# Splitting the third expert weights into fp16 pairs once, inside the attention loop, in place of once for every expert tile

## The chip, the cores and the metric

The kernel runs on one core of a Trainium2 chip. The metric is the device time of one execution in microseconds (us). The engines are named as in the profile: PE (matmul), PEld (PE's weight loads), DVE (vector), ACT (scalar), POOL (GpSimd) and SP, which here only issues DMAs. A name with q behind it (PEldq, SPq) is an engine's sequencer.

## The reference, cut to what matters

Two layers follow each other on x of 4 x 256 tokens x 256 features. The first mixes the features with a recurrence, then runs attention with 16 heads, then a mixture of 8 experts of which each token takes 2. The second mixes again and runs a quantised feed-forward block. The part that the change is about is the mixture:

```python
for e in range(E):                      # 8 experts, FF = 896, D = 256
    we = jnp.sum(gates * (top_idx == e), axis=-1)
    ye = jax.nn.silu(ht @ w1[e]) * (ht @ w3[e]) @ w2[e]
    out = out + we[:, None] * ye
```

The product with w2 is done in fp16 halves: 64 * w2 is cut into a high part, rounded to fp16, and a low part, the rest in fp16. The activations are cut likewise, and three of the four products of halves are added in PSUM.

## The kernel before

Every engine has its program written out by hand, in order, with semaphores between engines. The stages that matter here follow each other in time.

**Attention** (from about 113 to 310 us). `attention_steps` runs `step(u)` for u = 0 to 37 on PE, ACT, DVE and POOL. One step works on several units at once, a unit being a head for a pair of batches: in step u PE projects unit u (`proj`), makes the scores of unit u-2, transposes the probabilities of unit u-4 (`prob_transposes`), multiplies unit u-5 with its values (`weighted_values`) and projects unit u-6 out (`project_out`). ACT in step u does `exponentials(u-3)`, `pT_high(u-4)`, `swap_halves(KU+u)`, `o_high(u-5)`, in this order; DVE does `rope(KU+u)`, `normalise(u-3)`, `row_max(u-2)`, `pT_low(u-4)`, `o_low(u-5)`. PE's `proj` of step u+1 waits for `swap_halves` of step u, since both use the bank pb[0]. In steps 0 to 3 ACT and DVE also split wo.

**Routing** (to about 343 us), and then the **experts** (to about 580 us). The tokens are sorted into MT = 23 tiles of 128 slots; tile n belongs to expert e, read from a table in SBUF at run time (`tile_base`, `value_load`). The three weights of an expert lie as fp32 in one of RING = 3 places of `wreg`, loaded by `load_expert` on SP. For tile n PE does `up` (both first products, in two parts), `h_transposes(n-1)`, `x_transposes(n+1)` and `down(n-1)`. `w2_high` on ACT and `w2_low` on DVE split w2 of the tile's expert into `w2s`, for each of the 23 tiles, two buffers in turn. Beside its tile work DVE does pieces of the second layer's recurrence and of its weights (`beside_a`, `beside_b`), and POOL gathers rows and feeds the recurrence.

SP's own order is: the inputs, wo (after the first weights are split), `load_expert(0)` after wo is split, the stores of h2, experts 1 and 2, then the rest as tiles end.

Of the kernel before, what the change touches and what calls it, by code (L numbers as in the profile page):

```python
# [14 lines left out]
P = 128  # L15
# [23 lines left out]
SCALE = float(HD) ** -0.5  # L39
BLK = 3 * P  # L40
# [23 lines left out]
def build(nc, t, out):  # L64
    ctx = ExitStack()
    with ctx:
        def sb(name, shape, dt=F32):
            return ctx.enter_context(nc.sbuf_tensor(name, shape, dt))
# [54 lines left out]
        def recurrence_buffers(base):  # L123
# [14 lines left out]
        w2s = [[cut(region, at, FC * D // 2, F16).rearrange("p (c n) -> p c n", c=FC) for region, at in parts]  # L138
               for parts in (((areg, 4224), (areg, 5120)), ((areg, 6016), (breg, 5120)))]
# [83 lines left out]
        row_ids = sb("row_ids", [P, MT], I32)  # L223
        h2_dram = nc.dram_tensor("h2_dram", (NT * P, D), F32).ap()
# [22 lines left out]
            "hT_done hT_copied hTlo_done w2hi_done w2lo_done down_done y_copied "  # L247
# [18 lines left out]
        def load_expert(eng, e):  # L266

            base = (e % RING) * WEXP
            n = C * FF
            eng.dma_start(wreg[:, base:base + n].rearrange("p (c n) -> p c n", c=C),  # L270
                          t["L0_ffn_w1"][e].rearrange("(c p) n -> p c n", p=P)).then_inc(s_w[e % RING], 16)
            eng.dma_start(wreg[:, base + n:base + 2 * n].rearrange("p (c n) -> p c n", c=C),
                          t["L0_ffn_w3"][e].rearrange("(c p) n -> p c n", p=P)).then_inc(s_w[e % RING], 16)
            eng.dma_start(wreg[:, base + 2 * n:base + WEXP].rearrange("p (c n) -> p c n", c=FC),
                          t["L0_ffn_w2"][e].rearrange("(c p) n -> p c n", p=P)).then_inc(s_w[e % RING], 16)
# [9 lines left out]
        def _(sp):  # L285
# [25 lines left out]

            sp.wait_ge(s["wolo_done"], 4)
            load_expert(sp, 0)
# [49 lines left out]
        def _(pe):  # L363
# [229 lines left out]
            def down(n, parity, piece=None):  # L593
                pe.wait_ge(s["hTlo_done"], n + 1)
                pe.wait_ge(s["w2lo_done"], n + 1)
                if not isinstance(n, int) or n >= 1:
                    pe.wait_ge(s["y_copied"], n)
                if piece:
                    piece(pw)
                for c in range(FC):  # L600
                    last = split_products(pw[:, 0:D], lambda a: hhT[:, a, c, :], lambda a: w2s[parity][a][:, c, :], c == 0, c == FC - 1)
                last.then_inc(s["down_done"], 1)
# [12 lines left out]
            for n in range(MT + 1):  # L615
                parity = n % 2
                if n < MT:
                    e, base = tile_base(n)
                    pe.wait_ge(s["w_ready"], e + 1)
                    pe.wait_ge(s["xT_copied"], n + 1)  # L620
                    if n >= 1:
                        pe.wait_ge(s["inner_a_done"], n)
                    up(n, parity, base, 0)
                if n >= 1:
                    h_transposes(n - 1)
                if n + 1 < MT:
                    x_transposes(n + 1, (n + 1) % 4, x_slot.get(n))
                if n < MT:
                    up(n, parity, base, 1)
                if n >= 1:  # L630
                    down(n - 1, 1 - parity, y_slot.get(n))
# [58 lines left out]
        def _(act):  # L690
# [142 lines left out]

            def step(u, parity):
# [8 lines left out]
                if u < 4:  # L843
                    wo_high(u)
                if H + LAG + 1 <= u < H + LAG + 5:
                    squares_of_tile(u - H - LAG - 1)
# [51 lines left out]
            def w2_high(n, parity):  # L898

                e = act.value_load(tmi[0:1, bass.ds(n, 1)], min_val=0, max_val=NE - 1)  # L900
                act.wait_ge(s["w_ready"], e + 1)
                if not isinstance(n, int) or n >= 2:
                    act.wait_ge(s["down_done"], n)
                nc.scalar.activation(w2s[parity][0].rearrange("p c n -> p (c n)"),  # L904
                                     wreg[:, bass.ds((e % RING) * WEXP + 2 * C * FF, FC * D)], ACT.Copy, scale=WS).then_inc(s["w2hi_done"], 1)

# [6 lines left out]
            for n in range(MT + 1):  # L913
# [17 lines left out]
                if n < MT:  # L931
                    w2_high(n, parity)
# [57 lines left out]
        def _(dve):  # L990
# [186 lines left out]

            def second_norm(i):
# [4 lines left out]
            def step(u, parity):  # L1183
# [13 lines left out]
                if u < 4:  # L1197
                    wo_low(u)
                if H + LAG + 3 <= u < H + LAG + 7:
                    second_norm(u - H - LAG - 3)  # L1200
# [173 lines left out]
            def w2_low(n, parity):  # L1374

                e = dve.value_load(tmi[0:1, bass.ds(n, 1)], min_val=0, max_val=NE - 1)
                dve.wait_ge(s["w2hi_done"], n + 1)
                V.scalar_tensor_tensor(w2s[parity][1].rearrange("p c n -> p (c n)"),  # L1378
                                       wreg[:, bass.ds((e % RING) * WEXP + 2 * C * FF, FC * D)], WS,
                                       w2s[parity][0].rearrange("p c n -> p (c n)"), ALU.mult, ALU.subtract).then_inc(s["w2lo_done"], 1)  # L1380

# [14 lines left out]
            for n in range(MT):  # L1396
# [6 lines left out]
                w2_low(n, n % 2)  # L1403
# [287 lines left out]
```

## Time and profile before

| | |
|---|---|
| median of 3 runs | 705.23 us (705.21 to 707.87) |
| the profiled execution, its own time | 705.76 us |
| its span in the trace | 703.9 us |
| PE busy | 503.7 us |
| DVE busy | 539.9 us |
| ACT busy | 342.4 us |

The profiled execution took 705.76 us, of which the trace's span covers 703.9; some 1.9 us lie around it. Busy time is a sum over stages that have different limits, so it has to be read stage by stage.

### The profile page before, as it was taken

How to read it: one execution, taken by the hardware profiler on the slowest of the kernel's cores; microseconds unless marked ns; L12 is line 12 of the kernel's file. 1: busy time of each engine (PE TensorE's matmuls, PEld its weight loads, DVE VectorE, ACT ScalarE, POOL GpSimd, SP SyncE). 2: the span in 40 equal slices, each digit the busy share in tenths (PEclk: the TensorE clock that was granted, in tenths of full speed). 3: DMA queues.
4: the chain of work that ended last, by engine and by line, in shares of the span. 5: the costliest groups of instructions: out<-in, count | busy, mean ns of one | idle time of the engine just before them, and what ended most of it. 6: DMA issues, size and time to landing. Idle time of an engine off the chain costs nothing.

```text
span 703.9 us, 9187 instructions
## 1 busy us (share of the span) xinstructions
PE 503.7 (72%) x2954; PEld 342.0 (49%) x2954; DVE 539.9 (77%) x1004; ACT 342.4 (49%) x737; POOL 287.7 (41%) x232
## 2 busy tenths in 40 slices
PE   2011385799999999983589899999899980363442
PEld 1001132578888788863256566666566650132221
DVE  4999685788888889844288698787976853799983
ACT  3235154677777787830244645456255531342231
POOL 3454035644444455223534855332520004664250
PEclk9999999899999999995699999999999995555555
DMA  9200011400000000009216531604251002010000
GB/s 264 92 0 0 0 55 65 155 4 1 1 1 1 1 17 17 1 31 312 73 31 213 172 46 61 194 27 171 38 180 65 15 16 68 16 52 8 16 16 15
DMA packets 28314, 44.23 MB, mean 63 GB/s; under 512 B 4779, under 2 KB 21419, under 8 KB 28011
## 3 DMA queue, kind: packets, MB, share of 16 engines
q1 hardware_dynamic: 20843, 31.43, 13.8%
q0 software_dynamic: 3024, 8.14, 4.8%
q10 hardware_dynamic: 4400, 4.06, 1.7%
q8 instruction: 25, 0.41, 0.3%
q14 instruction: 22, 0.18, 0.1%
HBM read 38.51 MB, written 5.12 MB: 62 GB/s over the span
## 4 chain that ended last, share of the span: by engine, by line
PE 47%; DVE 30%; issue 10%; ACT 6%; POOL 5%; DMA 1%; SPq 0%; ACTq 0%; DVEq 0%; POOLq 0%
PE pb L405 9%; PE pw L405 9%; PE pb L581 6%; PE sc L444 6%; PE sc L581 5%; PE po L405 4%; PE pt L455 3%; DVE areg L1045 2%; DVE areg L1031 2%; DVE areg L1029 1%; PE pt L590 1%; POOL breg L1583 1%; DVE areg L1042 1%; DVE areg L1286 1%; DVE areg L1378 1%
## 5 line engine op out<-in xcount | busy, mean ns | idle before, releaser
L581 PE MATMUL pb<-wreg,areg 128*128 x184 | 84.8, 604 | 1.1 <-ACT areg L892 0.8
L1555 POOL TENSOR_TENSOR breg<-breg,con 128x512 f32<-128x512 f32 x32 | 40.7, 1270 | 82.9 <-ACT breg L794 82.9
L405 PE MATMUL pb<-areg,wreg 128*128 128x512 f16 x240 | 60.8, 391 | 14.8 <-ACT breg L794 9.4
L405 PE MATMUL pw<-areg 128*128 128x256 f16 x406 | 59.5, 283 | 8.7 <-DVE areg L1386 8.7
L581 PE MATMUL sc<-wreg,areg 128*128 x184 | 63.2, 486 | 0.0
L802 ACT ACTIVATE breg<-breg,mx 128x128 f32<-128x128 f32 (+1 forms) x128 | 56.6, 445 | 1.9 <-DVE mx L1153 1.7
L1597 POOL DMA_INDIRECT areg<-h_dram,row_ids x23 | 32.1, 1396 | 57.9 <-PE po L573 39.9
L581 PEld LDWEIGHTS pb<-wreg,areg 128*128 128x128 f32 x184 | 33.9, 195 | 36.5 <-issue 36.2
L405 PEld LDWEIGHTS pw<-areg 128*128 128x128 f16 x406 | 40.7, 101 | 19.3 <-DVE areg L1386 12.2
L444 PE MATMUL sc<-areg,breg 128*128 128x128 f32 (+1 forms) x256 | 49.5, 338 | 0.4 <-DVE mx L1153 0.4
L1550 POOL TENSOR_TENSOR breg<-breg 128x512 f32<-128x512 f32 x32 | 44.5, 1392 | 4.5
L444 PEld LDWEIGHTS sc<-areg,breg 128*128 128x128 f32 x256 | 40.1, 199 | 7.5 <-issue 1.6
L811 ACT CAST breg<-pt 128x768 f16<-128x768 f32 x32 | 25.5, 798 | 36.5 <-PE pt L455 36.5
L405 PEld LDWEIGHTS pb<-areg,wreg 128*128 128x128 f16 x240 | 22.2, 99 | 41.4 <-ACT breg L794 12.3
L581 PEld LDWEIGHTS sc<-wreg,areg 128*128 128x128 f32 x184 | 33.2, 190 | 18.3
L1153 DVE CUSTOM_DVE_ANT_0 breg<-sc,con 128x128 f32<-128x128 f32 (+1 forms) x128 | 38.1, 354 | 5.0 <-PE pt L455 2.0
L1372 DVE TENSOR_TENSOR areg<-areg,pb 128x512 f32<-128x512 f32 x23 | 15.7, 681 | 32.9 <-ACT areg L922 20.6
L922 ACT ACTIVATE areg<-pb 128x512 f32<-128x512 f32 x23 | 13.8, 598 | 54.6 <-PE pb L581 52.5
L1102 DVE TENSOR_TENSOR breg<-pb,con 128x512 f32<-128x512 f32 x40 | 27.5, 689 | 16.6 <-PE pb L405 14.1
L904 ACT ACTIVATE areg<-wreg 128x1792 f16 x23 | 39.6, 1724 | 0.0
L1643 POOL DMA_INDIRECT areg<-ys_dram,sloti x16 | 15.5, 967 | 55.0 <-DMA ys_dram<-areg 50.7
L382 PE MATMUL sc<-con,areg 128*128 128x128 f32 x16 | 4.5, 434 | 45.8 <-DVE areg L1048 45.8
(237 smaller groups left out, 1336.2 us busy)
## 6 DMA issues: line engine op xcount, KB each, us to landing
wreg<-in_L_ffn_w SPq DMA_DIRECT2D x24, 896.0 KB
ys_dram<-areg ACTq DMA_DIRECT2D x23, 128.0 KB
wreg<-in_L_ffn_wq SPq DMA_DIRECT2D x1, 2048.0 KB, 9.6
wreg<-in_L_ffn_wo SPq DMA_DIRECT2D x1, 2048.0 KB, 8.1
areg<-in_fside_BxSxS ACTq DMA_DIRECT2D x4, 256.0 KB, 5.9
x_in<-in_x SPq DMA_DIRECT2D x4, 256.0 KB, 4.1
h_dram<-areg SPq DMA_DIRECT2D x8, 128.0 KB, 1.9
out_dram<-areg SPq DMA_DIRECT2D x8, 128.0 KB, 1.7
```

Of the source, the lines that this page charges most:

```text
L405: last = nc.tensor.matmul(bank, w(a), m(b), start=first and k == 0, stop=final and k == 2)
L444: last = nc.tensor.matmul(sc2[:, b, o:o + w], qr[:, buf, b * S + qb * P:b * S + (qb + 1) * P], kT[:, kv, pair * PAIR + b * S:pair * PAIR + ...
L455: last = nc.tensor.transpose(pt2[:, b, k * P:(k + 1) * P], pr[:, buf, b, k * P:(k + 1) * P], ident)
L581: last = nc.tensor.matmul(bank, xsT[:, parity, c * P:(c + 1) * P], wreg[:, bass.ds(base + (m * C + c) * FF + lo, w)], start=c == 0, stop=c ...
L802: last = nc.scalar.activation(pr[:, parity, b, o:o + w], pr[:, parity, b, o:o + w], ACT.Exp, bias=mx[:, parity, k:k + 1], scale=-1.0, accu ...
L811: nc.scalar.copy(pT[:, parity, 0], pt2[:, :, 0:BLK]).then_inc(s["pThi_done"], 1)
L904: nc.scalar.activation(w2s[parity][0].rearrange("p c n -> p (c n)"), wreg[:, bass.ds((e % RING) * WEXP + 2 * C * FF, FC * D)], ACT.Copy, s ...
L1102: V.tensor_tensor(t1[:, parity, :].rearrange("p (b n) -> p b n", b=2), bank[:, :].rearrange("p (b n) -> p b n", b=2), rope_cos.rearrange(" ...
L1153: last = V.tensor_tensor_reduce(out=pr[:, parity, b, o:o + w], in0=sc2[:, b, o:o + w], in1=mask[:, o:o + w], scale=-SCALE, scalar=3e38, op ...
L1550: G.tensor_tensor(dst, t1[:, parity, :], t2[:, parity, :], ALU.add).then_inc(s["radd_done"], 1)
L1555: G.tensor_tensor(t2[:, parity, :].rearrange("p (b n) -> p b n", b=2), t2[:, parity, :].rearrange("p (b n) -> p b n", b=2), rope_sin.rearr ...
L1597: G.indirect_dma_start(out=xs[n % 4], out_offset=None, in_=h2_dram[:, :], in_offset=bass.IndirectOffsetOnAxis(ap=row_ids[:, n:n + 1], axis ...
```

## The change

w2 of all 8 experts is split before the experts begin. `W2_STEPS` names the attention steps 6, 8, ..., 20. In step 6 + 2e ACT makes the high half of expert e (`w2_high(e)`), at the end of its step; in step 7 + 2e DVE makes the low half (`w2_low(e)`), at the end of its step. There is one buffer for the fp32 weights (`w2_words`, in `areg`) and one for each half (`w2_half`). SP loads `w2_words` from DRAM, and stores both halves to the new DRAM tensor `w2_dram` once the low half is made; only behind these two stores does it issue the next expert's load. ACT waits for that load (`w2_in`) and for the two stores (`w2_out`) ahead of its next high half. `load_expert` takes the third weight as fp16 pairs from `w2_dram`, the same number of bytes as before, and `load_expert(0)` comes behind all of this on SP. In the expert tiles `w2_high` and `w2_low` are gone, and PE reads the halves where they lie in `wreg`, at an address that depends on the expert.

```diff
+W2_STEPS = tuple(range(6, 6 + 2 * NE, 2))
...
+        w2_words = cut(areg, 11264, FC * D)
+        w2_half = [cut(areg, at, FC * D // 2, F16) for at in (13056, 16896)]
...
-            eng.dma_start(wreg[:, base + 2 * n:base + WEXP].rearrange("p (c n) -> p c n", c=FC),
-                          t["L0_ffn_w2"][e].rearrange("(c p) n -> p c n", p=P)).then_inc(s_w[e % RING], 16)
+            eng.dma_start(cut(wreg, base + 2 * n, FC * D, F16).rearrange("p (s n) -> p s n", s=2), w2_dram[e])\
+                .then_inc(s_w[e % RING], 16)
...
+            for e in range(NE + 1):
+                if e >= 1:
+                    sp.wait_ge(s["w2lo_done"], e)
+                    for k in range(2):
+                        sp.dma_start(w2_dram[e - 1][:, k], w2_half[k]).then_inc(s["w2_out"], 16)
+                elif e == 0:
+                    sp.wait_ge(s["rat_done"], B)
+                if e < NE:
+                    sp.dma_start(w2_words.rearrange("p (c n) -> p c n", c=FC), t["L0_ffn_w2"][e].rearrange("(c p) n -> p c n", p=P))\
+                        .then_inc(s["w2_in"], 16)
             sp.wait_ge(s["wolo_done"], 4)
+            sp.wait_ge(s["w2_out"], 32 * NE)
             load_expert(sp, 0)
...
 # PE, down
-                pe.wait_ge(s["w2lo_done"], n + 1)
...
-                    last = split_products(pw[:, 0:D], lambda a: hhT[:, a, c, :], lambda a: w2s[parity][a][:, c, :], c == 0, c == FC - 1)
+                    last = split_products(pw[:, 0:D], lambda a: hhT[:, a, c, :],
+                                          lambda a: wreg[:, bass.ds(base + 2 * C * FF + (a * FC + c) * D // 2, D // 2)].bitcast(F16),
+                                          c == 0, c == FC - 1)
...
 # ACT
+            def w2_high(e):
+                act.wait_ge(s["w2_in"], 16 * (e + 1))
+                if e >= 1:
+                    act.wait_ge(s["w2_out"], 32 * e)
+                nc.scalar.activation(w2_half[0], w2_words, ACT.Copy, scale=WS).then_inc(s["w2hi_done"], 1)
...
+                if u in W2_STEPS:
+                    w2_high(W2_STEPS.index(u))
...
 # DVE
+            def w2_low(e):
+                dve.wait_ge(s["w2hi_done"], e + 1)
+                V.scalar_tensor_tensor(w2_half[1], w2_words, WS, w2_half[0], ALU.mult, ALU.subtract).then_inc(s["w2lo_done"], 1)
...
+                if u - 1 in W2_STEPS:
+                    w2_low(W2_STEPS.index(u - 1))
```

How the instructions stand, first on ACT, at the end of attention step 8. Before, `o_high` (the CAST out of po) is followed at once by the four ACTIVATE of the next step's `exponentials`; the CAST out of pt is `pT_high`, the two COPY are `swap_halves`:

```order
L817 CAST areg<-po 128x512
L802 ACTIVATE breg,sums<-breg,mx 128x128
L802 ACTIVATE breg,sums<-breg,mx 128x256
L802 ACTIVATE breg,sums<-breg,mx 128x128
L802 ACTIVATE breg,sums<-breg,mx 128x256
L811 CAST breg<-pt 128x768
L793 COPY breg<-pb 64x512
L794 COPY breg<-pb 64x512
```

After, with every line number higher:

```order
L833 CAST areg<-po 128x512
L854 ACTIVATE areg<-areg 128x1792
L818 ACTIVATE breg,sums<-breg,mx 128x128
L818 ACTIVATE breg,sums<-breg,mx 128x256
L818 ACTIVATE breg,sums<-breg,mx 128x128
L818 ACTIVATE breg,sums<-breg,mx 128x256
L827 CAST breg<-pt 128x768
L809 COPY breg<-pb 64x512
L810 COPY breg<-pb 64x512
```

The L854 row is `w2_high`, which waits for the load of `w2_words` and for the stores of the halves; the exponentials and both copies of the next step now stand behind it.

Then PE, in an expert tile. Before, between two parts of `up` (L581), the whole of `down` is one run of 21 matmuls, and the ISA rows, which work out an address in registers, stand only ahead of the matmuls of `up`:

```order
L581 ISA
L581 MATMUL sc<-wreg,areg 128x384
L405 MATMUL pw<-areg 128x256 x21
L610 TENSOR_LOAD tmi
L610 ISA x2
L619 REGISTER_ALU
L581 ISA
L581 MATMUL pb<-wreg,areg 128x512
```

After, the run of `down` (L418) has an ISA row ahead of two of every three matmuls, 14 in a tile; a piece of it and its end:

```order
L594 ISA
L594 MATMUL sc<-wreg,areg 128x384
L418 ISA
L418 MATMUL pw<-wreg,areg 128x256
L418 ISA
L418 MATMUL pw<-wreg,areg 128x256 x2
...
L624 TENSOR_LOAD tmi
L624 ISA x2
L635 REGISTER_ALU
L594 ISA
L594 MATMUL pb<-wreg,areg 128x512
```

What moved here: the reads of `down` go to `wreg`, and 14 register instructions joined PE's sequencer in each tile.

## Rows read from the trace of the kernel before

**Rows 1.** The page: busy time by engine.

```profile
PE 503.7 (72%) x2954; PEld 342.0 (49%) x2954; DVE 539.9 (77%) x1004; ACT 342.4 (49%) x737; POOL 287.7 (41%) x232
```

**Rows 2.** Windows: attention steps 6 to 21, two steps, the expert stage.

```profile
core 0: us, PE busy (x) PEld busy (x) DVE busy (x) ACT busy (x) POOL busy (x), PEclk, DMA share, GB/s
142.53:232.24 89.71, 89.56 (x706) 72.81 (x707) 74.91 (x225) 69.17 (x193) 41.01 (x33) 1.00 0.01 1
170.93:182.05 11.12, 11.12 (x90) 9.07 (x88) 9.32 (x28) 8.60 (x25) 5.07 (x5) 1.00 0.00 0
343.87:580.45 236.58, 224.04 (x1120) 142.38 (x1120) 184.29 (x198) 116.71 (x193) 85.47 (x61) 0.98 0.31 93
```

**Rows 3.** Timeline of ACT in one attention step (start, length, instruction).

```profile
171.17 0.40 ACT L802 ACTIVATE breg<-breg,mx 128x128 f32<-128x128 f32 x1
...
174.23 0.80 ACT L811 CAST breg<-pt 128x768 f16<-128x768 f32 x1 [1.20 <-PE pt L455]
...
176.25 0.58 ACT L817 CAST areg<-po 128x512 f16<-128x512 f32 x1
```

**Rows 4.** Timeline of DVE in the same step.

```profile
173.06 0.18 DVE L1134 RECIPROCAL sums<-sums 128x4 f32<-128x4 f32 x1
...
175.49 0.95 DVE L1160 TENSOR_TENSOR breg<-pt,breg 128x768 f16<-128x768 f32 x1
176.87 0.69 DVE L1164 TENSOR_TENSOR areg<-po,areg 128x512 f16<-128x512 f32 x1 [0.43 <-ACT areg L817]
```

**Rows 5.** The splits of w2, by their lines (ns min/median/max, first and last start).

```profile
L904 ACT ACTIVATE areg<-wreg x23: 1710/1721/1742, 351.5 to 570.2; 128x1792 f16 x23
L1378 DVE SCALAR_TENSOR_TENSOR areg<-wreg,areg x12: 2019/2026/3167, 354.8 to 573.2; 128x1792 f16<-128x1792 f16 x12
```

**Rows 6.** DMA issues (KB each, median us from issue to landing).

```profile
wreg<-in_L_ffn_wo SPq DMA_DIRECT2D x1, 2048.0 KB, 8.1
...
h_dram<-areg SPq DMA_DIRECT2D x8, 128.0 KB, 1.9
```

**Rows 7.** Windows: wo on its way (1 KB rows), then expert weights w1, w3 (3.5 KB rows).

```profile
106.00:107.00 1.00, 1.00 (x6) 0.41 (x6) 0.31 (x1) 0.45 (x1) 0.59 (x1) 1.00 1.09 362
136.00:137.00 1.00, 1.00 (x3) 0.30 (x2) 0.14 (x1) 1.00 (x6) 0.86 (x2) 0.50 1.01 412
```

**Rows 8.** Timeline of PE: waits, and two tiles without one.

```profile
361.36 2.47 PE L405 MATMUL pw<-areg 128*128 128x256 f16 x21 [1.68 <-DVE areg L1386]
402.74 3.77 PE L405 MATMUL pw<-areg 128*128 128x256 f16 x21 [3.34 <-DVE areg L1386]
433.07 0.28 PE L405 MATMUL pw<-areg 128*128 128x256 f16 x1 [0.54 <-DVE areg L1386]
443.44 0.33 PE L552 MATMUL pw<-identb,breg 88*128 88x88 bf16 x4 [0.90 <-DVE areg L1386]
465.02 3.60 PE L581 MATMUL pb<-wreg,areg 128*128 x8
474.31 3.60 PE L581 MATMUL pb<-wreg,areg 128*128 x8
491.75 0.28 PE L405 MATMUL pw<-areg 128*128 128x256 f16 x1 [0.54 <-DVE areg L1386]
503.84 4.13 PE L405 MATMUL pw<-areg 128*128 128x256 f16 x21 [2.62 <-DVE areg L1386]
```

**Rows 9.** Windows: a stretch with PE mostly idle, and the one behind it.

```profile
398.50:402.00 3.50, 0.89 (x3) 0.19 (x1) 1.17 (x2) 3.47 (x8) 3.12 (x3) 1.00 0.01 2
402.00:405.40 3.40, 2.66 (x13) 1.92 (x14) 3.37 (x4) 2.10 (x3) 3.09 (x3) 0.50 0.01 0
```

**Rows 10.** PE's sequencer in two tiles, and the start of one `down`.

```profile
L610 PEldq TENSOR_LOAD <-tmi x2: 298/302/305, 463.1 to 472.4; - x2
L581 PEldq FUSED_REGOPS  x12: 46/46/104, 463.9 to 473.8; - x12
...
472.02 0.27 PE L405 MATMUL pw<-areg 128*128 128x256 f16 x1
```

More of the change, by code:

```diff
@@ L136, in build @@
         hhT = cut(areg, 2816, FF, F16).rearrange("p (s c n) -> p s c n", s=2, c=FC)
-        w2s = [[cut(region, at, FC * D // 2, F16).rearrange("p (c n) -> p c n", c=FC) for region, at in parts]
-               for parts in (((areg, 4224), (areg, 5120)), ((areg, 6016), (breg, 5120)))]
+        w2_words = cut(areg, 11264, FC * D)
+        w2_half = [cut(areg, at, FC * D // 2, F16) for at in (13056, 16896)]
         ysb = cut(areg, 3712, 2 * D).rearrange("p (k n) -> p k n", k=2)
@@ L223, in build @@
         row_ids = sb("row_ids", [P, MT], I32)
+        w2_dram = nc.dram_tensor("w2_dram", (NE, P, 2, FC * D), F16).ap()
         h2_dram = nc.dram_tensor("h2_dram", (NT * P, D), F32).ap()
@@ L246, in build @@
             "w_ready xT_done xT_copied upa_done upb_done silu_a_done silu_b_done inner_a_done inner_b_done "
-            "hT_done hT_copied hTlo_done w2hi_done w2lo_done down_done y_copied "
+            "hT_done hT_copied hTlo_done w2_in w2_out w2hi_done w2lo_done down_done y_copied "
             "x1_ready sgx_ready qx_ready qxT_done qxT_copied gatep_done upp_done gate_ready gsig_ready up_ready p_ready "
@@ L591, in h_transposes, with down @@
                 last.then_inc(s["hT_done"], 1)
-            def down(n, parity, piece=None):
+            def down(n, base, piece=None):
                 pe.wait_ge(s["hTlo_done"], n + 1)
-                pe.wait_ge(s["w2lo_done"], n + 1)
                 if not isinstance(n, int) or n >= 1:
@@ L616, in _ @@
                 parity = n % 2
+                if n >= 1:
+                    last_base = base
                 if n < MT:
@@ L630, in _ @@
                 if n >= 1:
-                    down(n - 1, 1 - parity, y_slot.get(n))
+                    down(n - 1, last_base, y_slot.get(n))
             def quantised_transposes(i):
@@ L896, in _ @@
             copy_xT(0, 0)
[L898 to L905, printed above, removed]
             for k in range(2):
@@ L931, in _ @@
                 if n < MT:
-                    w2_high(n, parity)
                     act.wait_ge(s["upb_done"], n + 1)
@@ L1372, in silu @@
                 V.tensor_tensor(hh[:, lo:hi], silu_out[:, lo:hi], b, ALU.mult).then_inc(done, 1)
[L1374 to L1380, printed above, removed]
             def hT_low(n):
@@ L1402, in _ @@
                 silu(n, 1)
-                w2_low(n, n % 2)
                 if n in beside_b:
```

## The prediction

> **What bounds the kernel now.** I read the busy times of the page first, only to see that no engine limits the whole: PE has 72% and DVE 77% [rows 1]. The windows by stage say more [rows 2]. In attention steps 6 to 21 PE is busy 89.56 of 89.71 us, at the full clock (a granted clock of 1.00, the 2.4 GHz level). Over two steps it is busy 11.12 of 11.12 us, while ACT has 8.60 and DVE 9.32. So PE sets 5.56 us a step there, ACT has 1.26 us free a step and DVE 0.90. In the expert stage PE is busy 224.04 of 236.58 us, and DVE 184.29: PE again, with some 12.5 us of gaps. Two tiles without a gap start 474.31 - 465.02 = 9.29 us apart [rows 8]; 23 such tiles would be 213.7 us, so 22.9 us is all that lies above the barest tile, and part of that is PE's own work for the second layer.
>
> **What leaves the expert tiles.** 23 times 1.72 us of ACT and 23 times 2.03 us of DVE [rows 5], 39.6 and 46.6 us of busy time. Neither engine is the limit, so only PE's gaps count, those behind a DVE chain that holds a `w2_low` [rows 8]. The wait of 1.68 us at 361.36 ends with `hT_low(0)`, behind a `w2_low` of 2.03 on DVE: all of it goes, 1.7. The 3.34 at 402.74 goes back to POOL, whose gather waits for a DVE piece that three splits stand ahead of; POOL would start about 3.7 us earlier, of which the tiles themselves gained 1.7, so 2.0. The small waits, 0.54, 0.90 and 0.54, are shorter than one split: 2.0. The 2.62 at 503.84 lies behind a DVE that never rests and a split that took 3.17 (the longest in [rows 5]), so all goes, and with it the slow `down` behind it: 4.13 us where 2.47 is usual, 1.7, at half clock. Sum 1.7 + 2.0 + 2.0 + 4.3 = 10.0. The bounds are 5 (half of the gaps find another cause at once, above all POOL) and 16 (all 22.9 less the side pieces on PE).
>
> **What joins the expert tiles.** `down` gets 14 address computations a tile. One takes 46 ns on PE's sequencer [rows 10], 0.64 us a tile, 14.8 us in all if it showed. It is covered by the queue between sequencer and array: `down` begins on the array at 472.02, and the sequencer already loads the next tile's number at 472.4, so it had passed all 21 matmuls with about 1.9 us of array work to go. With 0.64 us more it still is ahead by about 1.2. Cost 0; without that cover, 0.64 us and the next tile's look-up of 0.30, for 22 tiles: the bound is 20. The third load has its old size, with longer rows: 0.
>
> **What joins attention.** By busy time the splits nearly fit: 1.72 in ACT's 2.52 free us of two steps, 2.03 against DVE's 1.80, a little over. What matters is the order. `w2_high(e)` needs `w2_words` filled again, and SP issues this load only when `w2_low(e-1)` has ended, behind two stores. That low half is the last thing of DVE's step 5 + 2e, and the high half the last of ACT's step 6 + 2e. DVE ends its step at 177.56 (`o_low`, 176.87 + 0.69) and ACT its own at 176.83 (176.25 + 0.58) [rows 3, 4], so ACT wants the weights 5.56 - 0.73 - 2.03 = 2.8 us after the low half. In this time 0.9 MB have to go out and 0.9 MB to come in.
>
> I build the loop from the end of `w2_high`, as time zero. The four exponentials take 1.89 us up to the reciprocal (171.17 to 173.06). From there to the end of `pT_low` are 3.38 (to 176.44). `o_low` adds 0.69, since `o_high` is done in time: the 0.43 that it waits for now is gone. Together 5.96, and `w2_low` 2.03: 8.0. Then the transfer: wo, 2.10 MB in the same 1 KB rows, landed in 8.1 us [rows 6], and moved 362 GB/s in mid-flight [rows 7]; 2.10 / 0.362 = 5.8, so 2.3 us are fixed. Now 0.917 MB goes out in 3.5 KB rows, which I price like the 3.5 KB rows of w1 and w3 at 412 GB/s, 2.2 us, and 0.917 MB comes in at 362, 2.5 us, in one queue: 2.3 + 2.2 + 2.5 = 7.0, and 0.1 for SP to wake, 7.1. With `w2_high` itself the loop is 8.0 + 7.1 + 1.8 = 16.9 us for two steps where PE needs 11.1. The rest of the loop is covered: ACT reaches the next high half at about 10.5 (the second step's rope waits for `w2_low` until 8.0) and stands still for some 4.7 us.
>
> **Who waits behind it.** Behind the waiting ACTIVATE stand the exponentials and `swap_halves` of the next step; PE's `proj` waits for the swap. PE still finishes one step, then idles 16.9 - 11.1 = 5.8 us a loop. Seven loops, for e = 1 to 7: 7 x 5.8 = 40.6. At the ends the first split delays its steps by about 3 us, and half comes back in steps 22 to 31, where DVE is slower than PE by little: 2.0. `load_expert(0)` moves from 132 us to behind step 21; it has over 60 us to land, so 0.
>
> For the transfer no row shows a store of this size. Below, the load without the stores would be 2.3 + 2.5 = 4.8, and I put the low end at 5.5. Above, both at half the rate make 2.3 + 9.4 = 11.7; the nearest store, 128 KB in 1.9 us [rows 6], has no such slowness, so I take 9.5. Each us is 7 us of the sum.
>
> The Trainium skill, "DMA: Bandwidth & Descriptors", section "Anatomy of one DMA", gives a DMA as about 2.0 us plus its bytes at 436 GB/s. By that the transfer would take 6.2 us, the loop 16.0 and the seven loops 34: an estimate from the page that is 6 us below mine, since wo moved slower than that here. The same section warns that a completion can be late when the target is HBM, which the stores here are. The 1.9 us of a 128 KB store does not bear that out, and no row shows it for 448 KB.
>
> **Sum.** 703.9 + 40.6 + 2.0 - 10.0 = 736.5 of span, 738.4 with the 1.9 us around it. The profiled execution was 0.5 above the median of its runs, so 738.
>
> **The rivals.**
> - *The transfers hide.* If one loop of DMA took 1.3 us or less (11.1 - 8.0 - 1.8), ACT would not wait, and attention would pay only DVE's 0.2 us for two steps, some 3 in all: 705.2 + 3 - 10 = 698, faster. Over it the loss grows by 7 us for each us, and the whole change breaks even near 2.4. Even 128 KB takes 1.9, and here it is fourteen times that. 3 in 100.
> - *Nearly even.* A short transfer (5.5, a loop of 15.3, so 7 x 4.2 = 29.4) and 16 gained in the tiles give 705.2 + 29.4 + 2 - 16 = 720.6, still 2% slower. For within 0.5% the loop would have to be near 13. 3 in 100.
> - *The clock.* When PE had been mostly idle for 3.5 us, the next 3.4 us ran at 0.50 [rows 9], the 1.2 GHz level. A loop has a gap of 5.8 us, so I expect such a stretch in each: it costs PE about 1.7 us of work, which the gap absorbs. If instead the clock stays low through the loop, PE's 11.1 us become up to 22 and PE sets the loop again: 7 x 11.1 - 10 = +68, 773. Against it, PE would be busy for 11 us on end, and the expert stage, which holds such a stretch, has a mean of 0.98 [rows 2]. 6 in 100.
> - *The sequencer shows.* PE's address work costs 0.3 to 0.9 us a tile: 745 to 758. 8 in 100.
> - *A slower or faster transfer.* At 9.5 us 755, at 5.5 us 727. 20 in 100 together.
> - The forecast itself, within 731 to 745: 60 in 100.
>
> **How the numbers follow.** The predicted time is the forecast's. The range takes both ends of the transfer and part of the gain's bounds: 724 to 757. It leaves out the hidden transfers, the even case and the low clock, 12 in 100, and some tails. A measurement of this kernel tells about 0.5%, or 3.5 us, from no change. Faster has the first rival's chance and a little for a gain that I don't see: 0.04; same 0.03; slower 0.93.
>
> **What would show it.** In the profile after: ACT's `w2_high` waits for a DMA seven times, for about 4.7 us each, near 33 in all. Attention's steps 8 to 21 come in pairs 16.9 us apart, at a PE busy share near 66%. The stores and the load land about 7 us after the low half. PE's waits in the expert stage fall from 12.5 to a few us, with `down` still at 2.3 us, and the stage takes about 227. The prediction is wrong if the pairs stay near 11 us, if the sequencer stretches `down` above 2.5 us, or if POOL keeps the gaps of the expert stage.

## The result: 6.1% slower, and where the time went

| | before | after |
|---|---|---|
| median of 4 runs | 706.55 us | 751.07 us (747.49 to 752.36) |
| the profiled execution, its own time | 705.76 us | 749.89 us |
| its span in the trace | 703.9 us | 748.1 us |
| start to the first tile's `up` | 343.87 us | 391.42 us |
| the expert stage | 236.58 us | 233.07 us |
| from its end to the end | 123.45 us | 123.61 us |

The ratio is 1.0614, with a 95% interval of 1.0555 to 1.0673. The span grew by 44.2 us: 47.55 ahead of the experts, -3.5 in their stage, 0.2 behind it. The forecast had 42.6, -10 and 0.

**The loop of two steps.** First the page's line of busy times, against [rows 1], then windows against [rows 2]: all seven loops (from 0.2 us ahead of the end of the first `w2_low` to just behind the end of the last), two single loops, and the expert stage.

```profile
PE 517.9 (69%) x2954; PEld 348.4 (47%) x2954; DVE 511.2 (68%) x989; ACT 320.3 (43%) x722; POOL 277.9 (37%) x232
```

```profile
core 0: us, PE busy (x) PEld busy (x) DVE busy (x) ACT busy (x) POOL busy (x), PEclk, DMA share, GB/s
160.86:282.46 121.60, 89.18 (x601) 68.18 (x599) 79.94 (x205) 70.69 (x174) 35.53 (x28) 0.87 0.32 107
161.06:178.02 16.96, 11.49 (x76) 8.25 (x75) 11.32 (x30) 9.41 (x24) 5.07 (x4) 0.90 0.32 108
178.02:196.17 18.15, 12.58 (x83) 9.45 (x81) 11.34 (x31) 10.21 (x25) 5.08 (x4) 0.82 0.30 102
391.42:624.49 233.07, 225.86 (x1120) 141.70 (x1120) 137.06 (x175) 81.75 (x170) 76.70 (x61) 0.99 0.30 94
```

Where PE was busy for all of 11.12 us, it now has 11.5 to 12.6 us of work in a loop of 17 to 18, some of it at half clock. The sums of busy time fell on DVE (28.7 us) and ACT (22.1 us), and the kernel got slower all the same: the work went, the order stayed in the way.

ACT's waits show the transfer, and the timelines of ACT and DVE the loop around it (start, length, instruction, and in brackets the idle time before it and what ended it). L854 is `w2_high`, L1194 `w2_low`:

```profile
ACT areg L854 <- DMA areg<-in_L_ffn_w: 29.8, 7, 5.4
```

```profile
168.07 1.70 ACT L854 ACTIVATE areg<-areg 128x1792 f16<-128x1792 f32 x1 [4.60 <-DMA areg<-in_L_ffn_w]
...
186.21 1.70 ACT L854 ACTIVATE areg<-areg 128x1792 f16<-128x1792 f32 x1 [5.41 <-DMA areg<-in_L_ffn_w]
203.24 1.70 ACT L854 ACTIVATE areg<-areg 128x1792 f16<-128x1792 f32 x1 [3.15 <-DMA areg<-in_L_ffn_w]
```

```profile
171.55 0.18 DVE L1148 RECIPROCAL sums<-sums 128x4 f32<-128x4 f32 x1 [5.57 <-ACT breg L818]
...
173.81 0.95 DVE L1174 TENSOR_TENSOR breg<-pt,breg 128x768 f16<-128x768 f32 x1
...
175.28 2.74 DVE L1194 SCALAR_TENSOR_TENSOR areg<-areg 128x1792 f16<-128x1792 f32 x1
```

From the start of `w2_high` to the start of `w2_low` are 175.28 - 168.07 = 7.21 us, and in the next loop again (186.21, and a `w2_low` at 193.42). `w2_low` takes 2.74. From its end at 178.02 to the next `w2_high` at 186.21 are 8.19 us, in the loops before and after it 7.01 and 7.07, over the seven 7.38 on average. 7.21 + 2.75 + 7.38 = 17.34 us, and the ends of the first and the eighth `w2_low` say the same: (282.41 - 161.06) / 7 = 17.34. Seven loops cost 7 x (17.34 - 11.12) = 43.5 us, and 4.0 of the 47.55 are left for the ends.

The chain that ended last, cut out around one transfer (start, length, what), names its parts; the groups of DMA issues (KB each, median us to landing) give their usual sizes:

```profile
175.36 2.67 DVE areg L1194
...
178.05 0.32 SPq L318
...
178.41 0.43 SPq L318
...
178.89 7.30 DMA areg<-in_L_ffn_w
```

```profile
areg<-in_L_ffn_w SPq DMA_DIRECT2D x8, 896.0 KB, 6.4
w_dram<-areg SPq DMA_DIRECT2D x16, 448.0 KB, 3.5
```

SP needs 0.85 us to issue both stores (L318), and then the load takes 6.4 as a rule.

PE waits behind it for the swap (ACT L810), in each loop. In four of the seven loops, after waits of 4.76 to 5.57 us, the first six matmuls then run at half clock, 2.74 us where 1.47 is usual. In the other three the wait was 3.31 to 4.04 us, and they take 1.47 to 1.57. Before the first loop and in it:

```profile
162.92 1.47 PE L418 MATMUL pb<-areg,wreg 128*128 128x512 f16 x6 [0.68 <-ACT breg L810]
...
173.45 2.74 PE L418 MATMUL pb<-areg,wreg 128*128 128x512 f16 x6 [4.79 <-ACT breg L810]
```

**The expert stage.** PE's waits in it, and its timeline over two tiles, against [rows 8]; L418 with x21 is `down`, L594 is `up`:

```profile
PE pb L594 <- issue: 1.9, 7, 0.5
PE pw L418 <- DVE areg L1398: 1.7, 3, 0.6
```

```profile
497.08 2.46 PE L418 MATMUL pw<-wreg,areg 128*128 x21
499.38 3.68 PE L594 MATMUL pb<-wreg,areg 128*128 x8
...
506.64 2.46 PE L418 MATMUL pw<-wreg,areg 128*128 x21
509.13 2.41 PE L594 MATMUL pb<-wreg,areg 128*128 x5
```

`down`'s waits for DVE are down to 1.7 us, as forecast, but a new releaser stands there, "issue", 1.9 us in 7 pieces, ahead of the first matmuls of `up`. This tile takes 509.13 - 499.38 = 9.75 us, with four small transposes of the second layer in it. The tile behind it has none of them: it ends with the next start at 518.81 and takes 9.68, where such a tile took 9.29 before. The starts of the tiles now lie 9.6 to 9.8 us apart nearly throughout, three of them 10.6 to 10.8; before, most lay 9.3 to 10.0 apart, by what the second layer adds to each, and three of them 11.2 to 14.3. The long tiles are gone, and each plain one has 0.3 to 0.4 us more. PE's sequencer shows why, against [rows 10]; L418 are the address computations of `down`, L624 is the look-up of the next tile's expert:

```profile
L418 PEldq FUSED_REGOPS  x28: 55/55/60, 506.0 to 517.6; - x28
```

```profile
L624 PEldq TENSOR_LOAD <-tmi x2: 299/304/308, 508.1 to 517.8; - x2
```

The first address of this `down` is worked out at 506.0 and the look-up begins at 508.1. Those 2.1 us hold 14 addresses and 21 weight loads with their matmuls, so each address takes some 0.15 us with the one or two pairs behind it. The look-up begins 1.5 us after the start of `down` (506.64), where it began 0.4 after it before. It ends too late for the first weight load of `up` to go ahead of its matmul: that load starts at 509.12, after 0.31 us in which PEld has nothing, and the matmul at 509.13. Before, they started at 474.20 and 474.31.

### The profile page after: what moved, and what is told of

The parts are those of the page before. It is cut to its first block, busy times and chain, and to the rows that moved or that the text cites. A ratio compares the mean times of both kernels' runs of the same rounds, so it can differ in the third digit from the quotient of the medians.

```text
span 748.1 us, 9271 instructions
## 1 busy us (share of the span) xinstructions
PE 517.9 (69%) x2954; PEld 348.4 (47%) x2954; DVE 511.2 (68%) x989; ACT 320.3 (43%) x722; POOL 277.9 (37%) x232
## 4 chain that ended last, share of the span: by engine, by line
PE 41%; DVE 28%; issue 11%; ACT 8%; DMA 7%; POOL 2%; SPq 1%; ACTq 0%; POOLq 0%; DVEq 0%
PE pb L594 9%; PE pw L418 8%; PE sc L594 7%; DMA areg<-in_L_ffn_w 6%; PE pb L418 5%; PE sc L457 3%; DVE areg L1194 3%; ACT breg L818 2%; PE pt L603 2%; DVE areg L1059 2%; PE po L418 2%; DVE areg L1045 1%; DVE breg L1167 1%; PE pt L468 1%; DVE areg L1043 1%
## 5 line engine op out<-in xcount | busy, mean ns | idle before, releaser
L418 PE MATMUL pb<-areg,wreg 128*128 128x512 f16 x240 | 66.2, 417 | 47.9 <-ACT breg L810 42.7
L418 PE MATMUL pw<-wreg,areg 128*128 (+2 forms) x699 | 89.9, 279 | 3.0 <-DVE areg L1398 1.7
L594 PE MATMUL pb<-wreg,areg 128*128 x184 | 86.2, 612 | 3.7 <-issue 1.9
L418 PEld LDWEIGHTS pw<-wreg,areg 128*128 128x128 f16 x699 | 68.1, 99 | 19.8 <-issue 6.5
L594 PE MATMUL sc<-wreg,areg 128*128 x184 | 63.2, 486 | 0.0
L418 PEld LDWEIGHTS pb<-areg,wreg 128*128 128x128 f16 x240 | 22.8, 103 | 78.2 <-ACT breg L810 47.4
L457 PE MATMUL sc<-areg,breg 128*128 128x128 f32 (+1 forms) x256 | 56.7, 374 | 0.6 <-DVE mx L1167 0.6
L594 PEld LDWEIGHTS pb<-wreg,areg 128*128 128x128 f32 x184 | 33.7, 193 | 43.0 <-issue 42.6
L457 PEld LDWEIGHTS sc<-areg,breg 128*128 128x128 f32 x256 | 45.9, 225 | 9.6 <-issue 3.0
L1608 POOL DMA_INDIRECT areg<-h_dram,row_ids x23 | 27.4, 1190 | 60.5 <-PE po L586 43.1
L1561 POOL TENSOR_TENSOR breg<-breg 128x512 f32<-128x512 f32 x32 | 43.5, 1360 | 4.5
L594 PEld LDWEIGHTS sc<-wreg,areg 128*128 128x128 f32 x184 | 33.2, 190 | 18.3
L937 ACT ACTIVATE areg<-pb 128x512 f32<-128x512 f32 x23 | 13.8, 599 | 62.7 <-PE pb L594 62.7
L418 PE MATMUL po<-breg,areg 128*128 128x256 f16 (+1 forms) x384 | 36.9, 246 | 0.3 <-DVE areg L1178 0.3
L1148 DVE RECIPROCAL sums<-sums 128x4 f32<-128x4 f32 x32 | 5.5, 172 | 45.9 <-ACT breg L818 45.4
```

Source lines behind the costliest of these rows:

```text
L418: last = nc.tensor.matmul(bank, w(a), m(b), start=first and k == 0, stop=final and k == 2)
L457: last = nc.tensor.matmul(sc2[:, b, o:o + w], qr[:, buf, b * S + qb * P:b * S + (qb + 1) * P], kT[:, kv, pair * PAIR + b * S:pair * PAIR + ...
L594: last = nc.tensor.matmul(bank, xsT[:, parity, c * P:(c + 1) * P], wreg[:, bass.ds(base + (m * C + c) * FF + lo, w)], start=c == 0, stop=c ...
L1561: G.tensor_tensor(dst, t1[:, parity, :], t2[:, parity, :], ALU.add).then_inc(s["radd_done"], 1)
L1608: G.indirect_dma_start(out=xs[n % 4], out_offset=None, in_=h2_dram[:, :], in_offset=bass.IndirectOffsetOnAxis(ap=row_ids[:, n:n + 1], axis ...
```

## Experiments

The ratio stands against the kernel before, timed beside them: 708.15 us for the first four, 706.79 for the next two, 706.28 for the last (medians). Where nothing is said of it, a kernel computes all of the reference.

**1. The transfers out of the way.** Two buffers for `w2_words` and two for the halves, in `areg` and in the free first place of `wreg`. SP loads expert e + 2 behind the stores of expert e, so each load has two steps of time.

```diff
-        w2_words = cut(areg, 11264, FC * D)
-        w2_half = [cut(areg, at, FC * D // 2, F16) for at in (13056, 16896)]
+        w2_words = [cut(areg, 11264, FC * D), cut(wreg, 0, FC * D)]
+        w2_half = [[cut(areg, at, FC * D // 2, F16) for at in (13056, 16896)],
+                   [cut(wreg, at, FC * D // 2, F16) for at in (FC * D, FC * D + FC * D // 2)]]
...
+            load_w2(0)
             sp.wait_ge(s["wolo_done"], 4)
+            load_w2(1)
+            for e in range(NE):
+                sp.wait_ge(s["w2lo_done"], e + 1)
+                for k in range(2):
+                    sp.dma_start(w2_dram[e][:, k], w2_half[e % 2][k]).then_inc(s_w2out[e % 2], 16)
+                if e + 2 < NE:
+                    load_w2(e + 2)
```

> The changed kernel with two buffers for the fp32 weights and two for each half, so that the load of expert e + 2 is issued when the low half of e is made, and ACT finds its weights there. The same splits, stores and tiles. Theory A (attention loses its time to the loop from the low half over the two stores and the load to the next high half, 17.3 us in place of 11.1): ACT's waits of 29.8 us go, a pair of steps falls to 11.4 to 12.1 us (DVE has 9.32 of 11.12 us of its own and 2.03 to 2.75 for the split), and the time falls from 751 to 704 to 711, about 708. Theory B (it is the splits' own work on ACT and DVE, or the clock, or the traffic): at least half of the loss stays, 730 or more.

Measured: 713.44 us, ratio 1.0083 (1.0048 to 1.0118). No `w2_high` waits for a DMA any more, and the experts begin at 356.01 instead of 391.42, 35.4 us earlier. So the wait for the transfer is 35.4 of the 47.55 us, which settles the main step. But the time misses theory A's 704 to 711, and a pair of steps its 11.4 to 12.1: 12.1 us of attention's loss are still there. A window of two steps (columns as above), and PE around it (L817 is the second copy of `swap_halves` in this kernel):

```profile
175.00:187.30 12.30, 11.48 (x90) 9.00 (x90) 11.36 (x30) 10.12 (x26) 5.12 (x5) 1.00 0.46 149
```

```profile
185.70 1.47 PE L425 MATMUL pb<-areg,wreg 128*128 128x512 f16 x6 [0.72 <-ACT breg L817]
...
197.99 1.47 PE L425 MATMUL pb<-areg,wreg 128*128 128x512 f16 x6 [0.72 <-ACT breg L817]
```

```profile
ACT breg L816 <- DVE breg L1123: 17.4, 11, 4.9
```

Two steps take 197.99 - 185.70 = 12.29 us, 1.17 over the old 11.12. The swap waits for DVE's rope (L1123), and the rope stands behind a `w2_low` of 2.76 us. Eight pairs at 1.17 are 9.4 of the 12.1.

**2. The addresses alone.** The kernel before, its splits still in every tile, but PE's `down` reads the halves through an address with a register in it. The register is always zero, so the same data are read.

```diff
+            def w2_at(parity, a, c):
+                region, at = (((areg, 4224), (areg, 5120)), ((areg, 6016), (breg, 5120)))[parity][a]
+                return region[:, bass.ds(zero + at + c * D // 2, D // 2)].bitcast(F16)
...
-                    last = split_products(pw[:, 0:D], lambda a: hhT[:, a, c, :], lambda a: w2s[parity][a][:, c, :], c == 0, c == FC - 1)
+                    last = split_products(pw[:, 0:D], lambda a: hhT[:, a, c, :], lambda a: w2_at(parity, a, c), c == 0, c == FC - 1)
...
+                    zero = e * none
```

> The kernel before, with the splits where they were; only, down reads its halves at an address that PE works out in registers (the offset is zero at run time), 14 address computations a tile as in the changed kernel. Theory A (the sequencer shows: in the changed kernel tiles without a wait start 9.7 us apart, not 9.29): tiles without a wait start 9.6 to 9.7 us apart, and the time is 6 to 9 us above the kernel before, about 712, a little less where PE waits for DVE anyway. Theory B (the 0.4 us of a tile come from something else of the change, as the place of the halves in wreg): within 1 us of the kernel before, 705 to 707.

Measured: 710.75 us, ratio 1.0057 (1.003 to 1.0083). The stage takes 240.73 us, 4.15 more than before. PE's waits, and two tiles:

```profile
PE pw L405 <- DVE areg L1392: 6.8, 5, 2.0
...
PE pb L581 <- issue: 2.4, 7, 0.5
```

```profile
466.00 3.70 PE L581 MATMUL pb<-wreg,areg 128*128 x8
...
475.68 3.70 PE L581 MATMUL pb<-wreg,areg 128*128 x8
```

The addresses alone bring the 9.68 us tile (475.68 - 466.00) and the "issue" ahead of `up`. That is theory A in kind. The size is missed: the medians differ by 2.6 us and the stage by 4.15, not by 6 to 9. Tiles that wait for a split hide a part, as `down`'s waits for DVE fell from 8.7 to 6.8 us. (The zero costs PE's sequencer one more operation of 32 ns in each tile.) The cost in the changed kernel is that of experiment 4.

**3. The load ahead of the stores.** As the changed kernel, but with two buffers for the halves alone, so that SP issues the next load first and the stores behind it.

```diff
+        w2_half = [[cut(areg, at, FC * D // 2, F16) for at in (13056, 16896)],
+                   [cut(wreg, at, FC * D // 2, F16) for at in (FC * D, FC * D + FC * D // 2)]]
...
-                    for k in range(2):
-                        sp.dma_start(w2_dram[e - 1][:, k], w2_half[k]).then_inc(s["w2_out"], 16)
...
+                if e >= 1:
+                    for k in range(2):
+                        sp.dma_start(w2_dram[e - 1][:, k], w2_half[(e - 1) % 2][k]).then_inc(s_w2out[(e - 1) % 2], 16)
```

> The changed kernel with one buffer for the fp32 weights as it has, but two for each half, so that the load of the next expert is issued ahead of the two stores, and ACT's high half does not wait for them. Theory A (the bytes of the stores are part of the loop): the transfer falls from about 7 to 5 us, seven loops lose about 2.2 us each, and the time is about 736. Theory B (the fixed latency is all of it, the stores run beside the load): 749 to 752.

Measured: 741.49 us, ratio 1.048 (1.0438 to 1.0523), between the theories. SP's timeline and the DMA groups:

```profile
160.73 0.37 SPq L322 DMA_DIRECT2D areg<-in_L_ffn_w  x1
...
176.60 0.38 SPq L322 DMA_DIRECT2D areg<-in_L_ffn_w  x1
```

```profile
w_dram<-areg SPq DMA_DIRECT2D x8, 448.0 KB, 7.1
```

```profile
areg<-in_L_ffn_w SPq DMA_DIRECT2D x8, 896.0 KB, 6.1
```

The load issues at once, 0.85 us earlier than in the changed kernel, and still takes 6.1 us where 6.4 was. The loop is 16.1 us on average (issues from 160.73 to 257.32 in six loops), and the experts begin 9.9 us earlier. So the time that SP spends issuing the stores is paid in full, and putting them behind the load saves only 0.3 us more. The stores now take 7.1 in place of 3.5 and run beside the load. What they cost it shows in a load that had none beside it, that of expert 1 in experiment 1, issued at 134.4:

```profile
L318 SPq DMA_DIRECT2D wreg<-in_L_ffn_w x1: 368/368/368, 134.4 to 134.4; - x1
...
DMA to landing us min/median/max: 5.1/5.1/5.1
```

It landed in 5.1 us, and the same load in experiment 5 as well. That is near my sum for a load without stores, 2.3 + 2.5 = 4.8. The stores add 1.0 to 1.3 us to the median load, whether they are issued ahead of it or behind it.

**4. The tiles without splits.** The kernel before, without the splits of tiles 2 to 22. `down` uses what tiles 0 and 1 left in the two buffers, so this kernel leaves that part of the computation out; `down`'s addresses stay fixed.

```diff
-                    w2_high(n, parity)
+                    if n < 2:
+                        w2_high(n, parity)
...
-                w2_low(n, n % 2)
+                if n < 2:
+                    w2_low(n, n % 2)
```

> The kernel before, which makes the split only for tiles 0 and 1 and leaves it out for the other 21, whose down reads what is there; nothing is split elsewhere, and the addresses of down stay fixed. It gives what leaving out the splits is worth to the expert stage alone. Theory A (my prediction: the waits of PE behind DVE go): the expert stage falls from 236.6 us by 10, the time to about 696. Theory B (POOL keeps the waits, and the changed kernel's stage was only 3.5 us shorter for that reason): about 702.

Measured: 697.77 us, ratio 0.9869 (0.9827 to 0.991). The stage takes 226.86 us, 9.7 less than before (its window, columns as above):

```profile
345.43:572.29 226.86, 221.07 (x1120) 141.28 (x1120) 140.81 (x177) 84.82 (x172) 77.46 (x61) 0.99 0.33 97
```

The sum of 10.0 that the prediction gave the removed splits is right, though this kernel keeps two splits and with them the wait of 1.68 us behind the first. Against the 233.07 of the changed kernel 6.2 us are left, with DVE and ACT as free in both. The two stages differ at their ends too: the changed kernel has no such wait, and its last `down` runs at half clock, 3.61 us in place of 2.46. From the start of the third tile to that of the last, where both are alike but for the addresses, are 191.49 us here and 197.77 in the changed kernel. That is 6.3 us over 20 tiles, 0.31 each. The changed kernels of experiments 1, 3 and 5, with the same `down`, have stages of 232.3 to 233.9 us.

**5. Quarters in place of wholes.** From experiment 1: each split is cut into four, one quarter in each of steps 4 to 35, ACT's behind the exponentials and DVE's behind `pT_low`, where neither is just ahead of the swap's chain.

```diff
-W2_STEPS = tuple(range(6, 6 + 2 * NE, 2))
+W2_FIRST, W2_PARTS = 4, 4
+W2_N = FC * D // W2_PARTS
...
+                if 0 <= u - W2_FIRST < W2_PARTS * NE:
+                    w2_high(u - W2_FIRST)
                 if within(u, 4):
...
                     pT_low(u - 4, parity)
+                if 0 <= u - W2_FIRST < W2_PARTS * NE:
+                    w2_low(u - W2_FIRST)
```

> The kernel of two buffers, with each split cut into four quarters, one quarter of a high and of a low half in each of the steps 4 to 35, and put where each engine idles: on ACT between the exponentials and pT_high, where it waits 1.2 us for PE in a step, on DVE between pT_low and o_low, where it waits 0.43 us for ACT. Two buffers alone still cost 1.16 us for two steps (12.28 in place of 11.12), with ACT and DVE waiting in turn. Theory A (that rest is whole splits in the path of the swap, which spread out fit in the idle time): a step comes back to 5.56 us, the experts start at 344 to 346 us, and the time falls from 713 to 702 to 704. Theory B (ACT and DVE have no such room, since each piece has a fixed cost and DVE and POOL get in each other's way): 708 or more.

Measured: 706.52 us, ratio 0.9989 (0.9962 to 1.0016). The experts begin at 346.18 us, 2.3 later than before, at the upper bound of theory A (346). The total is above its 702 to 704 by 2.5; the expert stage, untouched, takes 233.85 us where experiment 1 had 232.34, and the runs reach from 704.8 to 710.2, so I can't place the rest. The steps are back at 5.56 us:

```profile
181.94 1.46 PE L426 MATMUL pb<-areg,wreg 128*128 128x512 f16 x6
...
187.50 1.46 PE L426 MATMUL pb<-areg,wreg 128*128 128x512 f16 x6
```

The quarters are no cheaper in sum. By its line a quarter of the low half takes 1.32 us, more than a quarter of 2.75:

```profile
L1205 DVE SCALAR_TENSOR_TENSOR areg<-areg x16: 611/1322/1711, 136.1 to 290.8; 128x448 f16<-128x448 f32 x16
```

They have room all the same: DVE is busy for 11.05 us of the 11.12 of two steps. So of the 12.1 us of experiment 1 about 9.8 came from how the work was cut and placed, and not from how much it was. Size, place and the number of steps changed together; which of them counts most is not shown.

**6. The halves loaded for each tile.** From experiment 5: `load_expert` brings only w1 and w3. ACT loads the two halves of tile n's expert from `w2_dram` into the old places of `w2s`, behind its copy of y, so PE's addresses in `down` are fixed again.

```diff
+            def load_halves(n):
+                e = act.value_load(tmi[0:1, bass.ds(n, 1)], min_val=0, max_val=NE - 1)
+                for a in range(2):
+                    act.dma_start(w2t[n % 2][a], w2_dram[bass.ds(e, 1), :, a].rearrange("e p n -> p (e n)")).then_inc(s_w2t[n % 2], 16)
...
                     act.wait_ge(s["y_copied"], n)
+                    if n + 1 < MT:
+                        load_halves(n + 1)
```

> The kernel of quarters; only, the expert weights come without the third, and ACT's queue loads the two halves of the third weight for each tile (23 times 0.9 MB) into the fixed places that the kernel before used, so that down has fixed addresses again. Theory A (the address computations were worth what separates the expert stage of the changed kernel, 233.1 us, from that of the kernel without splits in the tiles, 226.9, of which 2 us more were waits behind the splits of its first two tiles): the stage is 225 to 227 us, and the time 7 us below the kernel of quarters, about 695. Theory B (the loads by tile arrive late or disturb, 21 MB over the stage, or ACT's issues delay its copies): the stage stays at 230 or more.

Measured: 712.33 us, ratio 1.0074 (1.0036 to 1.0112); the stage takes 241.28 us. Theory A's stage of 225 to 227 fell. The plain tile is back at 9.29 us, but five tiles take 11.2 to 15.1. ACT at two of its loads (L935):

```profile
390.10 0.85 ACTq L935 DMA_DIRECT2D areg<-w_dram  x2
...
391.57 0.60 ACT L954 ACTIVATE areg<-pb 128x512 f32<-128x512 f32 x1 [2.17 <-issue]
...
399.59 0.35 ACTq L935 DMA_DIRECT2D areg<-w_dram  x1
...
400.95 1.28 ACT L735 ACT_TABLE_LOAD   x1 [2.06 <-issue]
```

The number's load, the two issues and that of the store of y put 2.1 us between ACT's copy of y and its next work, the SiLU (L954) or the exponentials of the second layer with their table. In a tile that ACT is late in anyway, PE waits for it. The next experiment tests that reading, though not alone.

**7. One load a tile, in another place.** From experiment 6: the halves of a tile come in one DMA into one of three places by n % 3, issued while ACT waits for `up`'s second part.

```diff
+        w2t = [cut(wreg, k * WEXP + 2 * C * FF, FC * D, F16) for k in range(RING)]
...
-                for a in range(2):
-                    act.dma_start(w2t[n % 2][a], w2_dram[bass.ds(e, 1), :, a].rearrange("e p n -> p (e n)")).then_inc(s_w2t[n % 2], 16)
+                act.dma_start(w2t[n % RING], w2_dram[bass.ds(e, 1)].rearrange("e p a n -> p (e a n)")).then_inc(s_w2t[n % RING], 16)
...
+                    if n + 1 < MT and n >= 1:
+                        load_halves(n + 1)
                     act.wait_ge(s["upb_done"], n + 1)
...
-                    if n + 1 < MT:
-                        load_halves(n + 1)
```

> The kernel that loads the halves tile by tile, with three fixed places in wreg (the rooms of the third weights that the ring no longer needs) in place of two, one DMA a tile in place of two, issued one tile ahead where the high split of a tile stood before, in ACT's wait for the second part of up. In the last kernel ACT's number load and two issues, 2.1 us a tile, stood between the copy of y and the next SiLU, and tiles with exponentials took 13.3 to 15.1 us. Theory A (that place of the issues made the new waits): tiles without side pieces start 9.3 us apart, the expert stage falls from 241.3 to 225 to 229 us, and the time to 696 to 699, 1% below the kernel before. Theory B (the traffic itself, 21 MB more in the stage, delays POOL's gathers): the stage stays at 235 or more and the time at 705 or more.

Measured: 698.34 us, ratio 0.9886 (0.9866 to 0.9906), faster than both kernels. The stage as a window, and where one `up` (L602) follows `down` (L426):

```profile
347.57:574.27 226.70, 222.54 (x1120) 142.25 (x1120) 136.79 (x175) 81.76 (x170) 76.49 (x61) 0.98 0.54 170
```

```profile
478.78 2.46 PE L426 MATMUL pw<-wreg,areg 128*128 128x256 f16 x21
481.07 3.60 PE L602 MATMUL pb<-wreg,areg 128*128 x8
```

226.70 us is the stage of experiment 4, with all of the computation in it, and from the third tile to the last are 191.53 us, as there. `up` follows `down` after 2.29 us again (481.07 - 478.78), not after 2.49 as at 506.64. The 13.8 MB more that are loaded delay nothing that shows: DMA's share rises from 0.30 to 0.54, and PE's tiles are no longer. Three things changed at once against experiment 6, the place of the issue, one DMA for two and three buffers for two, so what each gives is not shown.

## Why the prediction was right, and where it was off

The direction and the mechanism held, and 751.07 lies in the range, in its upper half, but outside the 731 to 745 to which I gave 60 in 100. The upper part of the range was there for a slow transfer of 9.5 us. The transfer took 7.38, and what filled that part was mostly a term that I had put at 0, the addresses. That the range held is in part luck. The span came out 11.6 us above the sum (748.1 against 736.5). By terms:

- **The loop of 16.9 us: 17.34 measured.** Seven loops cost 43.5 instead of 40.6. Its parts were off in both directions. From the start of `w2_high` to that of `w2_low` I had 1.8 + 5.96 = 7.8, it is 7.2: the reciprocal starts 171.55 - 169.77 = 1.78 after the split's end, not 1.89, `pT_low` ends 3.21 after it, not 3.38, and `w2_low` starts 0.52 behind that, not 0.69. The transfer was 7.1 and is 7.38. Experiment 1 shows that it is the cause: without it 35.4 us go. Its parts were 4.8 for the load, 2.2 for the stores' bytes and 0.1 for SP. They came out as 5.1 for a load alone (experiment 1), 1.3 that the stores add to it (6.4 in the changed kernel), and 0.85 for issuing them, which experiment 3 wins back. The sum is near, but a good part of what I gave to bytes is issue time.
- **`w2_low` at 2.03 us: 2.75 measured.** This is the mis-sized term of the loop, 0.72 x 7 = 5.0 us. I took its time from the expert tiles, where POOL mostly does other things. In attention it meets the sum that ends POOL's part of the rope (L1561), in all eight loops. POOL's timeline beside the split at 175.28:

```profile
174.88 1.27 POOL L1561 TENSOR_TENSOR breg<-breg 128x512 f32<-128x512 f32 x1
```

  POOL ends at 176.15, 0.87 us after the split's start, and 2.74 - 0.87 = 1.87 is near the 2.03 of a split that nothing holds up. The first split starts at 158.14 and takes 2.92; POOL's sum there ends at 159.18, 1.04 after its start, and again 1.88 are left. The split of 3167 ns in [rows 5] is the same thing: it starts at 497.35, and POOL has an addition from 497.34 to 498.62 there. The Trainium skill says it in "SBUF — State Buffer", section "Who interferes with whom": a DVE instruction with two SBUF inputs contends with a GpSimd instruction that reads SBUF, and the port pair that they share is an exclusive lock. These times agree with it.
- **"DVE's 0.2 us for two steps", if transfers hide.** This failed. Experiment 1 hid them and each pair still cost 1.17 us, as the split is 2.75 and stands in the swap's way. With that and the addresses, the rival at 698 really stands at 713. Only with the work cut and put elsewhere (experiment 5) is attention nearly free.
- **"With 0.64 us more it still is ahead by about 1.2. Cost 0."** This is the step that failed. I priced an address as its own 46 ns and took 1.9 us for the sequencer's lead over the array. An address takes 55 ns here, but the sequencer needs 2.1 us for the run of `down`, and the look-up starts 1.5 us into it instead of 0.4. So the lead shrinks by 1.1 us and not by 0.64. What is left of the lead doesn't cover the look-up and `up`'s first addresses and weight loads. It costs 0.31 us a tile, and 6.2 us between the stages of experiment 4 and of the changed kernel. `down` itself stays at 2.46 to 2.49 us, so my sign for it, a `down` above 2.5, did not catch it. The rival "The sequencer shows", at 0.3 to 0.9 us a tile, had the kind of it and the lower end of its size.
- **The tiles' gain of 10.0: 9.7,** by experiment 4. The sum is right and its items are not. The gap that I put down to POOL, 3.34 us and a slow `down` behind it, gives 4.2 where I had 2.0: 0.43 and a `down` of 2.47 us are left. Of the small waits, 2.0 by my sum, 1.08 stay in experiment 4, and in the changed kernel `down` still waits three times for DVE, 0.45, 0.60 and 0.61 us. So "POOL keeps the gaps" did not happen, but two of the small waits did not hang on a split. Net of the addresses 3.5 are seen.
- **The ends at 2.0: 4.0 measured,** what 7 loops leave of the 47.55. The traces place 2.4 of them ahead of the first split of w2: PE's projection of step 6 starts at 144.96 in place of 142.53. DVE's third split of wo, at nearly the same time in both kernels, takes 2.27 us behind POOL's sum and 1.22 ahead of it. First the changed kernel, then the one before:

```profile
126.45 2.27 DVE L1190 SCALAR_TENSOR_TENSOR wreg<-wreg 128x1024 f16<-128x1024 f32 x1
```

```profile
126.53 1.22 DVE L1176 SCALAR_TENSOR_TENSOR wreg<-wreg 128x1024 f16<-128x1024 f32 x1
```

  In the first POOL's sum had started at 126.36, in the second it started at 126.68. In experiment 4, whose attention is that of the kernel before, the same split takes 2.26, and step 6 starts at 144.86. So this delay happens without the change too, when POOL is first; how 1.05 us grow to 2.4 by step 6 is open. 1.6 are left for the change, near my 2.0. But nothing "comes back" in steps 22 to 31: the projections of steps 23 and 31 are both 47.87 us late.
- **The clock.** The half-clock stretch came right after the gap in four loops of seven, not in each, and did not stay: PE's mean clock in the loops is 0.87. It makes PE busy for longer, so that its share is 89.18 / 121.60 = 73%, not 66%. ACT's waits add up to 29.8 us, not 33; ACT reaches its next split later than I had it, for which I have no experiment.

The errors of 2.9 (loops), 2.0 (ends), 6.5 (tiles: 6.2 and 0.3) and 0.2 make the 11.6. The Trainium skill's sum for a DMA, "DMA: Bandwidth & Descriptors", section "Anatomy of one DMA", was too low for the transfer as a whole: 6.2 us against 7.38. The page fits it to DMAs that GpSimd issues, and these are issued by SP. For one store of 448 KB it gives about 3.1 us, an estimate from the page; the stores, issued in pairs, show 3.0 to 3.1 in experiment 1 and 3.5 in the changed kernel.

## What to carry to other kernels

Work that is moved out of a tight stage into a roomy one must fit its order and not only its idle time: a single buffer that goes out and in between two engines' turns makes a loop, and the loop's length, not any busy share, sets the time. Two buffers and small pieces placed off the critical chain took the cost of attention from 47.6 to 2.3 us. And an address that depends on a register takes more of the sequencer's lead than its own nanoseconds, and it shows wherever the next look-up waits behind it. Loading the data to a fixed place, with more bytes and one DMA a tile issued in a wait, made the stage 7 us shorter than in experiment 5.

## What the runs showed of the hardware that was not expected

- DVE and POOL hold each other up here: a split that takes 2.03 us by itself takes 2.75 or 2.92 when POOL's sum is under way at its start, and 3.17 when both start together. It goes both ways. In experiment 5 the median quarter took 1.32 us. One that came first took 0.61, and then POOL's sum took 1.64 where 1.27 is its usual length; timelines of DVE and POOL:

```profile
239.13 0.61 DVE L1205 SCALAR_TENSOR_TENSOR areg<-areg 128x448 f16<-128x448 f32 x1
```

```profile
239.24 1.64 POOL L1572 TENSOR_TENSOR breg<-breg 128x512 f32<-128x512 f32 x1
```

- Fourteen address computations of 55 ns, 0.77 us by themselves, put the look-up behind them about 1.1 us later, and made the tile 0.31 us longer.
- On ACT, one register load, two DMA issues with a register in the address and a plain store kept the engine from its next instruction for 2.1 us.
- A load of 0.9 MB landed in 5.1 us alone, and in 6.1 to 6.4 us (medians) beside two stores of half its size, whether it was issued behind them or ahead of them.
